# New engine orders for the attention half pairs of a causal attention and mixture-of-experts kernel

## The reference

```python
K = einsum('bpd,ihd->biph', xn, W_K)      # Q and V alike
scores = where(tril, einsum('biph,biqh->biqp', K, Q), NEG_INF)
attn = softmax(scores / sqrt(64), axis=-1)
z = einsum('biph,biqp->biqh', V, attn)
attention = einsum('bqf,df->bqd', z_flat, W_O)
hidden = silu(xn @ Wg[e]) * (xn @ Wu[e]);  experts = sum_e cw[e] * (hidden @ Wd[e])
out = x + attention + experts
```

## Time and profile before

| | |
|---|---|
| median of the runs | 730.27 us (729.05 to 731.67) |
| the profiled execution | 729.04 us |
| its span, first to last instruction | 727.2 us |
| mean granted TensorE clock | 0.983 |
| busy: PE, PEld | 693.7 us (95%), 601.1 us (83%) |
| busy: DVE, ACT, POOL | 629.2 us (87%), 549.7 us (76%), 486.1 us (67%) |

### The profile page before, as it was taken

The page is one execution under the profiler, slowest core; times in us unless marked ns, Lnnn a source line. Parts: engine busy times, 40 slices in busy tenths (PEclk is TensorE's granted clock), DMA queues, the critical chain, the costliest instruction groups (busy, mean ns, idle before and its releaser), DMA issues.

```text
span 727.2 us, 14967 instructions
## 1 busy us (share of the span) xinstructions
PE 693.7 (95%) x4845; PEld 601.1 (83%) x4845; DVE 629.2 (87%) x1401; ACT 549.7 (76%) x1280; POOL 486.1 (67%) x494
## 2 busy tenths in 40 slices
PE   7879999899999999999999999999999999999997
PEld 7769999777888888888888888888888888888786
DVE  7977767678998899999898999998989999988886
ACT  4745555568888888888788888887888888888873
POOL 5274444157778776868787768687868676878761
PEclk8779999999999999999999999999999999999999
DMA  8514622142424242424242424242515151525101
GB/s 237 164 29 116 163 72 59 42 99 59 101 67 105 52 106 55 106 51 106 63 106 55 109 49 107 50 106 66 118 39 127 35 122 36 117 46 128 29 2 58
DMA packets 50235, 61.03 MB, mean 84 GB/s; under 512 B 7440, under 2 KB 28272, under 8 KB 50160
## 3 DMA queue, kind: packets, MB, share of 16 engines
q1 hardware_dynamic: 47856, 55.36, 32.1%
q0 software_dynamic: 2304, 4.72, 2.6%
HBM read 12.87 MB, written 4.72 MB: 24 GB/s over the span
## 4 chain that ended last, share of the span: by engine, by line
PE 76%; DVE 11%; ACT 4%; DMA 3%; POOL 3%; issue 2%; SPq 1%
PE ps_big L1381 18%; PE ps_mid L1416 15%; PE ps_z L1436 7%; PE ps_z L1437 7%; DVE neg_max L1105 4%; PE ps_misc L1244 4%; PE ps_misc L1246 3%; PE ps_misc L1245 3%; DMA k_st<-k_st 3%; PE ps_big L1334 3%; ACT probs L847 2%; PE ps_big L1378 2%; PE ps_z L1358 2%; PE ps_z L1359 2%; PE ps_big L1335 2%; PE ps_big L1336 2%
## 5 line engine op out<-in xcount | busy, mean ns | idle before, releaser
L687 POOL TENSOR_TENSOR probs<-probs,rden 128x1024 f32<-128x1024 f32 (+7 forms) x256 | 290.7, 1148 | 134.6 <-DVE rden L1140 133.7
L860 ACT ACTIVATE pT_hi<-ps_mid 128x512 fp32r<-128x512 f32 (+3 forms) x384 | 181.6, 491 | 67.1 <-PE ps_mid L1416 63.9
L1105 DVE TENSOR_REDUCE neg_max<-ps_big 128x1 f32<-128x1024 f32 (+7 forms) x256 | 192.4, 752 | 35.5 <-PE ps_big L1381 31.3
L1381 PE MATMUL ps_big<-k_st,q_st 128*128 128x512 f32 (+2 forms) x768 | 208.1, 379 | 4.7 <-ACT probs L847 3.0
L1151 DVE TENSOR_TENSOR pT_lo<-ps_mid,pT_hi 128x512 fp32r<-128x512 f32 (+3 forms) x384 | 203.6, 545 | 6.0 <-ACT pT_hi L860 2.3
L847 ACT ACTIVATE probs<-ps_big,neg_max 128x1024 f32<-128x1024 f32 (+7 forms) x256 | 189.9, 742 | 17.8 <-DVE neg_max L1105 15.2
L1416 PE MATMUL ps_mid<-ident,probs 128*128 128x128 f32 x1152 | 177.4, 275 | 9.5 <-DVE pT_lo L1151 7.2
L1416 PEld LDWEIGHTS ps_mid<-ident,probs 128*128 128x128 f32 x1152 | 136.2, 141 | 37.0 <-issue 15.2
L1381 PEld LDWEIGHTS ps_big<-k_st,q_st 128*128 128x128 f32 x768 | 119.2, 194 | 11.5 <-ACT probs L847 4.0
L1436 PE MATMUL ps_z<-pT_hi,v_st 128*128 128x256 f32 x448 | 118.6, 297 | 0.0
L1437 PE MATMUL ps_z<-pT_lo,v_st 128*128 128x256 f32 x448 | 112.0, 282 | 0.0
(11 more groups left out here) (243 smaller groups left out, 1263.2 us busy)
## 6 DMA issues: line engine op xcount, KB each, us to landing
k_st<-k_st SPq DMA_DIRECT2D x90, 256.0 KB, 3.7
q_st<-q_parts SPq DMA_DIRECT2D x128, 128.0 KB, 3.1
y_dram<-y_sb SPq DMA_DIRECT2D x40, 64.0 KB
k_st<-k_parts SPq DMA_DIRECT2D x8, 256.0 KB
raw_gu<-in_L_ffn_Wg_dram SPq DMA_DIRECT2D x9, 176.0 KB, 2.8
raw_gu<-in_L_ffn_Wu_dram SPq DMA_DIRECT2D x9, 176.0 KB, 2.9
raw_d<-in_L_ffn_Wd_dram SPq DMA_DIRECT2D x9, 128.0 KB, 2.9
res<-in_L_attn_x_dram SPq DMA_DIRECT2D x4, 256.0 KB, 3.8
```

The lines of the kernel that those rows point to most:

```text
L687: pool.tensor_tensor(rows, rows, col.to_broadcast([P, width]), ALU.mult).then_inc(normed, 1)
L860: nc.scalar.activation(pT_hi[:, t:t + 2 * tiles - 1:2, :], ps_mid[:, bank, 0:tiles * P].rearrange("p (t q) -> p t q", t=tiles), ACT.Copy). ...
L1105: nc.vector.tensor_reduce(neg_max[:, n:n + 1], ps_big[:, n % 2, off:off + width], AX_X, ALU.max, negate=True).then_inc(max_done, 1)
L1381: ins = nc.tensor.matmul(ps_big[:, n % 2, c0:c1], w, k_st[half][h][:, part, c0 - off:c1 - off], start=part == 0 and not masked, stop=part ...
```

## The change

All four order tables are written anew. The steps in them are the same, one for one; their order, and the half to which some belong, is not. In the old table v0 and v1 stand in the second half of the row, v2 and v3 at its end; in the new one v0, v2, v3 and v1 stand between the fourth and the eighth unit, with two V pieces of the half before (V5, V6, V7) ahead of them. Keys, queries and weights of the next half come earlier: q1 and k1 near the head of the row, and wqkv, k0 and q0 at the end of the row before (they now carry a "+"). k0 comes first and k1 last of the key parts. On VectorE the cast of k0 (`Ck0+`) stands behind R14 and ahead of L11.0, the cast of k1 behind R5; on GpSimd K0 stands behind N4 and K1 behind N6, where they were behind N8 and N4. `MISC_ORDER` and `TURN_AT` follow. The steps of the last half are hung on other steps, and TensorE's wait for `y_done` (the experts' last sum) moves ahead of the attention's first product, since products now reach into the time before half 0.

```diff
         PE_ORDER = read("""
-            T15.0- S4 T0.0 T0.1 Mwqkv V6.0- V6.1- T1.0 V6.2- Mk1 T2.0 T2.1 S5 Mq0 S6 V7.0- T3.0 V0.0 S7 T4.0 Mq1
-            S8 S9 T4.1 V0.1 V0.2 Mk0 T5.0 S10 T6.0 Mv0 S11 V1.0 T6.1 Mo1- T7.0 T8.0 S12 V2.0 T8.1 Mo0- V2.1 T9.0
-            S13 S14 T10.0 T10.1 Mv1 V3.0 V3.1 T11.0 S15 S0+ T12.0 T12.1 V4.0 S1+ V4.1 Mwo T13.0 T14.0 S2+ Mv2
-            T14.1 V5.0 S3+ V5.1 Mv3""")
+            V5.0- S3 V5.1- Mq1 T15.0- S4 T0.0 T0.1 S5 V6.0- V6.1- T1.0 V6.2- T2.0 S6 T2.1 Mk1 V7.0- S7 T3.0 Mv0
+            T4.0 S8 V0.0 T4.1 Mv2 S9 V0.1 T5.0 Mv3 T6.0 S10 V0.2 S11 T6.1 Mo1- V1.0 T7.0 Mv1 S12 T8.0 V2.0 T8.1
+            Mo0- V2.1 T9.0 S13 Mwo S14 V3.0 Mwqkv+ T10.0 T10.1 S15 V3.1 Mk0+ T11.0 T12.0 S0+ Mq0+ T12.1 V4.0 S1+
+            V4.1 T13.0 S2+ T14.0 T14.1""")
         ACT_ORDER = read("""
...
-            H5.0 E9 H6.0 Cv0 H6.1 E10 H7.0 E11 H8.0 H8.1 E12 H9.0 Z0 E13 H10.0 H10.1 E14 H11.0 Z1 Cv1 E15 H12.0
-            H12.1 E0+ Cwo H13.0 E1+ H14.0 Cv2 H14.1 E2+ H15.0""")
...
+            Cv2 E8 Y1- H5.0 Cv3 E9 H6.0 Y0- E10 H6.1 H7.0 Cv1 E11 H8.0 H8.1 E12 H9.0 Cwo E13 Z0 Cwqkv+ H10.0
+            H10.1 E14 Ck0+ H11.0 E15 H12.0 Z1 H12.1 E0+ H13.0 E1+ Cq0+""")
         DVE_ORDER = read("""
-            L15.0- R1 Cv3- X4 R2 L0.0 Cwqkv L0.1 R3 R4 L1.0 Z2- Ck1 X5 L2.0 L2.1 X6 Cq0 X7 Z3- R5 R6 L3.0 X8 Cq1
-            L4.0 X9 R7 L4.1 Ck0 X10 R8 L5.0 Cv0 L6.0 L6.1 X11 Co1- R9 R10 L7.0 X12 L8.0 Co0- L8.1 R11 R12 X13 L9.0
-            X14 L10.0 R13 Z0 R14 L10.1 X15 L11.0 X0+ Cv1 L12.0 L12.1 R15 X1+ Z1 Cwo R0+ L13.0 X2+ Cv2 L14.0 L14.1
-            X3+""")
+            Cq0 L14.0- X3 L14.1- R1 L15.0- R2 X4 Cq1 L0.0 L0.1 R3 X5 L1.0 R4 Z2- X6 L2.0 L2.1 X7 R5 Ck1 R6 L3.0
+            Cv0 X8 L4.0 L4.1 R7 Cv2 X9 Z3- R8 L5.0 Cv3 X10 L6.0 Co1- X11 R9 L6.1 L7.0 Cv1 X12 R10 L8.0 R11 Co0-
+            L8.1 R12 X13 L9.0 Cwo X14 R13 Cwqkv+ L10.0 L10.1 X15 Z0 R14 Ck0+ L11.0 X0+ R15 L12.0 X1+ L12.1 Z1
+            L13.0 X2+ R0+""")
         POOL_ORDER = read("""
-            N1 N2 N3 N4 K1 Z1- N5 N6 N7 Z0- N8 K0 N9 N10 N11 N12 N13 N14 N15 N0+""")
+            N1 N2 N3 N4 K0 N5 N6 K1 Z1- N7 N8 Z0- N9 N10 N11 N12 N13 N14 N15 N0+""")
...
-        MISC_ORDER = ["wqkv", "k1", "q0", "q1", "k0", "v0", "o1", "o0", "v1", "wo", "v2", "v3"]
+        MISC_ORDER = ["wqkv", "k0", "q0", "q1", "k1", "v0", "v2", "v3", "o1", "v1", "o0", "wo"]
...
+            pe.wait_ge(y_done, SUBS)
             for p in range(-1, PAIRS + 1):
                 if p == 0:
                     pe.wait_ge(pads_zero, 1)
-                    pe.wait_ge(y_done, SUBS)
                 iteration(p)
```

More of the change, by code:

```diff
@@ L311, in bass_layernorm_causal_attention_plus_moe_kernel @@
-            H12.1 E0+ Cwo H13.0 E1+ H14.0 Cv2 H14.1 E2+ H15.0""")
+            H14.0- H14.1- E2 H15.0- Cq1 E3 H0.0 H0.1 E4 H1.0 Z2- H2.0 E5 H2.1 Ck1 E6 H3.0 Cv0 H4.0 E7 Z3- H4.1
+            Cv2 E8 Y1- H5.0 Cv3 E9 H6.0 Y0- E10 H6.1 H7.0 Cv1 E11 H8.0 H8.1 E12 H9.0 Cwo E13 Z0 Cwqkv+ H10.0
+            H10.1 E14 Ck0+ H11.0 E15 H12.0 Z1 H12.1 E0+ H13.0 E1+ Cq0+""")
         DVE_ORDER = read("""
-            L15.0- R1 Cv3- X4 R2 L0.0 Cwqkv L0.1 R3 R4 L1.0 Z2- Ck1 X5 L2.0 L2.1 X6 Cq0 X7 Z3- R5 R6 L3.0 X8 Cq1
@@ L317, in bass_layernorm_causal_attention_plus_moe_kernel @@
+            L13.0 X2+ R0+""")
         POOL_ORDER = read("""
-            N1 N2 N3 N4 K1 Z1- N5 N6 N7 Z0- N8 K0 N9 N10 N11 N12 N13 N14 N15 N0+""")
-        MISC_ORDER = ["wqkv", "k1", "q0", "q1", "k0", "v0", "o1", "o0", "v1", "wo", "v2", "v3"]
+            N1 N2 N3 N4 K0 N5 N6 K1 Z1- N7 N8 Z0- N9 N10 N11 N12 N13 N14 N15 N0+""")
+        MISC_ORDER = ["wqkv", "k0", "q0", "q1", "k1", "v0", "v2", "v3", "o1", "v1", "o0", "wo"]
         OUTS = [int(n[1]) for n in MISC_ORDER if n[0] == "o"]
         LAST = (PAIRS - 1, 1)
-        TURN_AT = {"k1": (1, 1), "q0": (1, 0), "wo": (0, 1), "v2": (0, 0)}
+        TURN_AT = {"k0": (1, 1), "q0": (1, 0), "v1": (0, 1), "wo": (0, 0)}
@@ L902, in iteration @@
                             round_last({"0": 0, "1": 1, "2": 4, "3": 5}[arg])
-                        if kind == "C" and arg == "wo":
+                        if kind == "H" and arg == "14.0":
                             round_last(2)
-                        if kind == "C" and arg == "v3":
+                        if kind == "H" and arg == "15.0":
                             round_last(3)
@@ L1205, in iteration @@
                             add_x(*TURN_AT[arg])
-                        if kind == "C" and arg == "wo":
+                        if kind == "L" and arg == "14.0":
                             split_last(2)
+                        if kind == "L" and arg == "15.0":
+                            split_last(3)
                         if kind == "Z" and arg in "01":
@@ L1510, in iteration @@
             def iteration(p):
-                last_misc[:] = [bank_read(at, b, arg) for kind, arg, at, b, live in steps(PE_ORDER, p - 1) if kind == "M" and live][-1:]
                 for kind, arg, at, b, live in steps(PE_ORDER, p):
@@ L1515, in iteration @@
                             fill_twice()
-                        if kind == "M" and arg == "v2":
-                            last_out(0)
                         if kind == "M" and arg in TURN_AT:
                             turn_sum(*TURN_AT[arg])
-                        if kind == "V" and arg == "6.0":
+                        if kind == "V" and arg == "5.0":
+                            last_out(0)
+                        if kind == "T" and arg == "15.0":
                             last_out(1)
-                        if kind == "V" and arg == "6.2":
+                        if kind == "V" and arg == "6.1":
                             last_out(2)
```

2 lines of the change are left out of this document (removed).

## The result

The kernel with the new orders takes **704.62 us** (median; 701.6 to 705.3) where the kernel before takes 730.71 on the same chip: ratio **0.9637**, 95% interval 0.9603 to 0.9672. The forecast was 719.0 with a range of 711 to 731: right in sign, but it had 11.3 us of gain where 26.1 were measured. The profiled execution takes 701.60 us with a span of 699.8, where before had 729.04 and 727.2. Lines of TensorE are one higher than before (L1382 the scores, L1417 the transposes, L1437 and L1438 the products with V, L1245 to L1247 the products M).

What follows compares the result with a forecast made beforehand. The prediction took TensorE to be the bound, busy 98% of every window. From 729.0 us, -14.8 stalls, +4.2 k0's cast and -0.6 entrance gave 717.8; the median, 1.2 above the profiled execution, made 719.0, range 711 to 731.

Steps and rivals of the forecast that it cites:

- The dense price: TensorE's stretch without stalls: 33.1 us per half without V, 36.0 with; 517.6 in all, leaving 20.8 of stalls.
- The 0.13 per score step: In the dense price, 0.13 us for each of 16 score steps, by which their starts are further apart.
- The allowance: Stalls left in the new order: 0.4 us per half (bounds 0.2 and 1.0); 20.8 becomes 6.0, -14.8 us.
- The cast of k0: VectorE's cast behind R14 races GpSimd's norm N14: wins by 0.08 us; if it loses, 1.05 us per half.
- 4 of 14 blocked: Number of k0 casts assumed to lose to norm N14, at 1.05 us each: +4.2 us.
- k1's cast gains up to 0.7 per half, hidden: Behind R5 the cast starts ahead of N5; VectorE is spared up to 0.7 us per half, hidden.
- The waits named ahead of T11.0, o1 and S0: TensorE's idle 0.40 us before T11.0 and 0.36 before o1 gone; S0 never behind a key DMA.
- S0 to T0.0: Entrance: later E0 and N0 in half 0 put the first transpose at 148.8 instead of 147.26, +1.5 us.
- the moved products: k0, q0 and q1 of the first half run before its first transpose: 2.1 us leave the dense stretch.
- The end: The last half's closing chain has the same steps in the same order: 0, bounds +-1 us.
- Blocked casts: Rival: most k0 casts lose to N14, 14 x 1.05 = 14.7 in place of 4.2, giving 729.5 us; chance 0.17.
- VectorE as the bound: Rival: VectorE 93% busy, in-order waits bring 1.0 us per half back, 15.0 for 6.0, 728.0 us; chance 0.13.

Runs made afterwards that it cites:

- light_after: The changed kernel with row maximum and norm over 128 columns only (output not the reference's): ratio 0.9511 to the kernel before, stretch 506.17 us.
- blocked: The changed kernel with R14 ahead of Z0 on VectorE, so norm N14 starts before k0's cast: ratio 0.9814 to the kernel before, stretch 526.03 us.
- light_before: The kernel before with row maximum and norm over 128 columns only (output not the reference's): ratio 0.9655 to the kernel before, stretch 520.05 us.
- extra_max: The changed kernel with one more 512-column row maximum ahead of units 7 and 14, result unused: ratio 0.9758 to the kernel before, stretch 521.86 us.
- casts_moved: The kernel before with k1's cast behind R5, k0's behind R8, and GpSimd's K1 behind N5: ratio 1.0573 to the kernel before.
- three_moves: The kernel before with K0 ahead of Z0 and N8, S15 ahead of T11.0 and unit 2's exponential ahead of H14.1 together: ratio 1.023, stretch 554.35 us.
- three single repairs: The kernel before with one move each: K0 ahead of Z0 and N8, S15 ahead of T11.0, unit 2's exponential ahead of H14.1: ratios 1.0141, 1.0014, 1.0089.

## Why the prediction was wrong, by its own steps

**The dense price failed; it is the largest term.** It put the stretch's floor at 517.6 and so the old order's stalls at 20.8. light_after ran the stretch in 506.17, or 507.2 with what moved counted back: the floor is at least 10.4 us lower and the stalls were **31.3**. Two errors make this up.

The first is a count, 3.7 us. Half 0 was priced as a full half with V, but no half stands before it: the trace has no output product in it (6 x 0.23) and 60 products with V for 80 (20 x 0.118), before and after alike.

The second is the price of a half, 6.7 us over the stretch. The halves without V take 32.22 and 33.13 in light_after (priced 33.13), those with V 35.24 and 35.56 (36.08). By kind of step, as start distances per half without V: transposes 6.71 (priced 7.85), products of V 10.0 (9.44), scores 11.23 (11.55), six products 4.46 (4.14), so 0.6 too much in all. Steps overlap at their borders, so one kind's gain is partly its neighbour's loss, and only the sum tells. The largest entry is the last transpose of a group: the prediction's own row said that it costs 0.03 ahead of a product, and the sum still has all 72 transposes at 0.109, 24 of them the last of a group. Of the 1.1 us that this is too much, 0.9 come back in the products behind. The 0.13 per score step is 0.11 in light_after. Together the two errors are a third of the stalls that the sum was about.

**The allowance was right.** 0.4 us per half, 6.0 in all, was left to the new order; it has 6.3 above light_after.

**The cast of k0 was placed rightly and priced rightly, and then hedged away.** Walked: the cast wins by 0.08; measured 0.11, between 0.10 and 0.12 in all 14 halves (0.427 to 0.43 us each). Price if it loses: 1.05, measured 0.97. The +4.2 for "4 of 14 blocked" was the wrong step: with the same steps in each half the race came out one way in all 14, in the new order as in blocked, and by the walk the likelier value was 0. The error of the walk was 0.03, not 0.1. The floor, the hedge and the small surplus over the allowance make the whole miss in the stretch: 10.4 + 4.2 - 0.3 = 14.3, which is 24.9 - 10.6.

**"k1's cast gains up to 0.7 per half, hidden" was wrong in the word hidden.** The casts cost the old order 5.9 us, most of it behind k1's, and the new one 0.5. It isn't a further part of the miss: in the sum it lies within the stalls of the old order, which the prediction had too small.

**The steps that held.** The waits named ahead of T11.0, o1 and S0 went, as forecast, and of the four places where light_before and light_after differ the prediction had listed three: T11.0, o1 (behind T6.1) and S4 (behind T15.0). The fourth, behind T6.0, it had not; in the halves without V the next step there is S11, and light_before shows TensorE 8 times behind an exponential, 2.0 us in all. S0 to T0.0 took +1.84 (forecast +1.5), and the moved products -2.07 (-2.1). The end took -0.94 (0 +- 1), but not for the reason given, the same steps in the same order: ten of its transposes had moved into the stretch. The halves are 35.2 to 35.6 and 32.7 to 33.7, not 36.4 and 33.6. The granted clock, 0.54 from 147.3 to 150.0 in the earlier trace rows, is 1.00 in the same place in after, where TensorE has products to do in the wait for the first probabilities; this was left as it was in the forecast, and lies within half 0's gain of 2.07.

**The rivals.** Blocked casts: the mechanism exists at its price, 717.0 when provoked, and didn't occur. VectorE as the bound: it would have needed more work than it has; extra_max shows that each microsecond more costs half of one. That a single wait could be mended in the old order, which the experiments asked and not the prediction, fell in all three, and with them the sum of the three.

**What stays open.** Of the 18.4 - 6.3 = 12.1 us of load-dependent gain, the casts' removal accounts for at most 5.4; the other 6.7 are put down to wider distances, by difference and not by a run. The split is the old order's: in the new one a late cast of k0 alone costs 13.5 (blocked), so distances and casts are not independent. The shares of the single moves in the new table can't be given, since single moves don't add up (casts_moved, three_moves).

## What to carry to other kernels

Get the floor of an order-bound stretch from a run in which the neighbours' work is cut: here the prices of the kinds of step, each near the truth by itself, added up to 0.6 us too much per half. Count the first and the last pass by themselves, for what they lack and what is moved into them. A race between two engines that repeats in each pass came out the same in all 14 here; forecast all or none, and then provoke the other case once for its price. When one wait is taken out of a hand-written order of queues, look for who stands behind the moved step on every queue, SyncE's DMAs among them: here three single repairs gained nothing or lost up to 10 us in the stretch, the three together lost 16, the casts' new place alone 40, and the joint order gained 25.

## What the runs showed of the hardware

- A busy TensorE hides stalls: before, the idle time in the table of waits is 9.6 us in the stretch, the stalls by start distances are 31.3 against light_after.
- A transpose ahead of an fp32 product costs 0.03 us by start distance, and the product's own distance to its successor is 0.32 in place of 0.23; ahead of the bf16 mask it costs its full 0.109. T6.1 and o1 of half 8, then T10.0 with T10.1 and S15 of half 9, in after (six transposes take 0.65 to the mask, where the earlier trace rows has 0.57 to a product):

```profile
439.51 0.27 PE L1417 MATMUL ps_mid<-ident,probs 128*128 128x128 f32 x1
439.53 0.48 PE L1245 MATMUL ps_misc<-z_hi,wo_hi 128*128 128x512 f32 x1
439.85 0.39 PE L1246 MATMUL ps_misc<-z_hi,wo_lo 128*128 128x512 f32 x1
440.08 0.39 PE L1247 MATMUL ps_misc<-z_lo,wo_hi 128*128 128x512 f32 x1
...
476.33 0.82 PE L1417 MATMUL ps_mid<-ident,probs 128*128 128x128 f32 x6
476.98 0.22 PE L1379 MATMUL ps_big<-causal_bf,ident_bf 128*128 128x128 bf16 x1
```

- A norm that starts 0.10 to 0.12 behind VectorE's cast takes 2.06 to 2.08 us for 1.89, less than the 0.32 of the cast that is left. In light_after the norm of 128 columns behind the cast takes 0.57 to 0.59 where light_before has 0.40, so the price is near 0.18 for the long norm and the short one. The other way round the cast ends 0.28 behind the norm, however long before the norm had started (29 of the 30 casts in before, 14 in blocked).
- SyncE's queue spends 0.59 to 0.66 us on each small DMA (the chain of casts_moved above), so the eleven between k1's low part and k0's move take 7.9 us. k1's transfer of 3.94 us landed within 0.1 us of the end of the four copies issued behind it, so there the queue lost next to nothing by waiting for it.
